# Delta stage: the seven-tap filter moved from VectorE to ScalarE and GpSimd, and the stage's order planned anew

## The reference, cut to what matters

```python
q, k, v = (silu(conv4(x @ W.T)) for each of the three)        # 4 heads of 32
delta_out = delta_rule_chunkwise(l2norm(q), l2norm(k), v * beta)   # chunks of 32 tokens
firs = [_dwconv_causal(vflat, f) for f in (fir_w3, fir_w7, fir_w15, fir_w31)]
branches = jnp.stack(firs + [v, delta_out], 0)                # six branches
stats = mean(abs(branches), -1)                               # one number per token, head, branch
h1 = gelu([x, stats] @ gate_w1.T + b1);  logits = h1 @ gate_w2.T + b2 + alpha * stats
probs = softmax(logits / temp) with a floor on the last branch
o = sum over branches of branch * prob;  o = rmsnorm(o);  x = x + o @ o_proj.T
```

## Time and profile before

| what | value |
|---|---|
| three executions | 3999.51, 4001.47, 4015.3 us (median 4001.47) |
| profiled execution, own time | 3997.58 us |
| its span | 3995.8 us, 88226 instructions |
| mean granted TensorE clock over the span | 0.865 |
| busy over the span | PE 82%, DVE 70%, ACT 58%, POOL 31% |

### The profile page before, as it was taken

One profiled execution on the slowest core, in us unless ns is written; L12 is line 12 of the kernel. 1 busy time (PEld: TensorE's weight loads), 2 busy tenths in 40 slices (PEclk: granted clock), 3 DMA queues, 4 the chain that ended last, 5 costly groups with the idle time before them and its releaser, 6 DMA issues. The chain is left out here.

```text
span 3995.8 us, 88226 instructions
## 1 busy us (share of the span) xinstructions
PE 3288.4 (82%) x36384; PEld 1507.5 (38%) x36384; DVE 2804.5 (70%) x4300; ACT 2329.8 (58%) x3893; POOL 1238.3 (31%) x1018
## 2 busy tenths in 40 slices
PE   5999999899767777699888888887995676876798
PEld 1222222266411112256533333333453555555444
DVE  8898899587689998887633776764436568657642
ACT  3888788676555555366432466665655565444564
POOL 1100100055447767555523000001003565453100
PEclk7999999899867778799989999997996676656799
DMA  4101010100010100100155011101000000000000
GB/s 100 28 9 28 19 22 4 36 2 2 11 32 16 32 16 16 48 1 2 27 61 68 18 30 30 33 23 52 1 1 11 4 4 3 4 4 3 30 1 22
DMA packets 138340, 85.14 MB, mean 21 GB/s; under 512 B 94578, under 2 KB 109731, under 8 KB 137811
## 3 DMA queue, kind: packets, MB, share of 16 engines
q1 hardware_dynamic: 135190, 75.24, 9.0%
q0 software_dynamic: 2688, 4.20, 0.7%
q10 hardware_dynamic: 64, 0.07, 0.0%
HBM read 47.49 MB, written 18.60 MB: 17 GB/s over the span
## 5 line engine op out<-in xcount | busy, mean ns | idle before, releaser
L949 DVE TENSOR_REDUCE attn_peak_halves<-attn_ps 128x2 f32<-128x1024 f32 x512 | 601.6, 1219 | 61.6 <-PE attn_ps L780 53.8
L902 ACT ACTIVATE attn_weights<-attn_ps 128x512 f32<-128x512 f32 x1024 | 531.1, 601 | 104.6 <-PE attn_ps L808 104.5
L2901 DVE TENSOR_REDUCE sparse_peak<-sparse_ps 128x4 f32<-128x1024 f32 x256 | 309.3, 1223 | 134.1 <-PE sparse_ps L2531 132.5
L1205 POOL TENSOR_TENSOR moe_hidden<-moe_exact,moe_hidden 128x512 f16<-128x512 f32 x256 | 297.0, 1164 | 329.3 <-ACT moe_hidden L1189 320.8
L3577 POOL TENSOR_TENSOR delta_q<-delta_q,delta_weighted 128x512 f32<-128x512 f32 x240 | 323.6, 1376 | 236.7 <-ACT delta_weighted L3971 236.3
L2761 ACT ACTIVATE sparse_weights<-sparse_ps 128x512 f32<-128x512 f32 (+1 forms) x512 | 272.0, 585 | 176.8 <-PE sparse_ps L2598 89.3
L246 PE MATMUL moe_ps<-moe_xT_halves,moe_w_halves 128*128 128x512 f16 x1536 | 363.6, 383 | 9.2 <-DVE moe_w_halves L1222 5.9
L808 PE MATMUL attn_ps<-attn_q_stack,attn_k_stack 50*128 50x512 f16 x1024 | 321.8, 386 | 33.7 <-ACT attn_weights L902 7.1
L1716 POOL TENSOR_TENSOR mamba_out_c<-mamba_states,mamba_c_rep 128x1024 f32<-128x1024 f32 x128 | 301.5, 2366 | 153.4 <-DVE mamba_states L1782 125.2
L246 PE MATMUL ffn_ps<-ffn_layers,ffn_h_halves 128*128 128x512 f16 x1536 | 334.5, 379 | 3.6 <-ACT ffn_gate L3130 3.6
L1506 PE MATMUL mamba_ps<-mamba_stack,mamba_spread 96*128 96x512 bf16 x512 | 197.3, 495 | 159.2 <-ACT mamba_decays L1670 85.0
(11 more groups left out here) (477 smaller groups left out, 6371.6 us busy)
## 6 DMA issues: line engine op xcount, KB each, us to landing
mamba_stack<-mamba_parts SPq DMA_DIRECT2D x96, 128.0 KB, 2.4
sparse_factor<-sp_factor SPq DMA_DIRECT2D x24, 256.0 KB, 3.8
sp_halves<-sparse_parts SPq DMA_DIRECT2D x8, 512.0 KB, 2.9
ffn_h<-in_h SPq DMA_DIRECT2D x4, 1024.0 KB, 7.7
attn_q_stack<-attn_halves SPq DMA_DIRECT2D x96, 32.0 KB
attn_k_stack<-attn_halves SPq DMA_DIRECT2D x96, 32.0 KB
attn_halves<-attn_hp SPq DMA_DIRECT2D x8, 384.0 KB, 3.3
attn_q_stack<-attn_peak_rows SPq DMA_DIRECT2D x128, 2.0 KB
```

The lines of the kernel that those rows point to most:

```text
L902: act.activation(weights[:, at % 2, h, :], use.slot, ACT.Exp).then_inc(*key_act.one())
L949: dve.tensor_reduce(peak_halves[:, turn % PEAKS, keys, at:at + 2], use.slot, AX_X, ALU.max).then_inc(*score_dve.one())
L1205: pool.tensor_tensor(low, exact_sb[:, i % 3, :], hidden[:, i // EB % 3, i % EB, 0, :], ALU.subtract).then_inc(*hidden_low.one())
L2901: dve.tensor_reduce(peak[:, at % PEAKS, unit // 2, 4 * r:4 * r + 4], use.slot.rearrange("p h (a k) -> p (h a) k", a=2), AX_X, ALU.max).the ...
```

## The change

The seven-tap filter (n = 1) leaves `TAP_ORDER`, so DVE makes the filters of 3 and 15 taps alone, 18 instructions for a sequence. `BY_POOL = (LONG, 1)` and `POOL_TAPS` put it behind the long filter in ACT's chain of scalings and POOL's chain of additions: 38 taps for a sequence in place of 31. Its first tap is written by ACT straight into `branch`, the other six go through `weighted` and POOL. The first scaling of the seven-tap filter waits for the last `sources` and the last absolute value of the sequence before. In `STAT_ORDER` branch 1 moves from the third place to the fifth. `URGENCY` goes from 0.004 to 0.002, and `AHEAD` gets other entries, so the order of all pieces of the stage is planned anew.

```diff
-TAP_ORDER = [(k, n) for k in range(max(FIR_TAPS)) for n, count in enumerate(FIR_TAPS) if n != LONG and k < count]
-STAT_ORDER = [4, 0, 1, 2, 3, 5]
+BY_POOL = (LONG, 1)
+POOL_TAPS = [(n, k) for n in BY_POOL for k in range(FIR_TAPS[n])]
+
+TAP_ORDER = [(k, n) for k in range(max(FIR_TAPS)) for n, count in enumerate(FIR_TAPS) if n not in BY_POOL and k < count]
+STAT_ORDER = [4, 0, 2, 3, 1, 5]
...
-URGENCY = 0.004
-AHEAD = {"kept": 1.5, "root": 1.5, "sums": 0.5, "norm_root": 0.5, "uw": 0.5, "raw": 2, "hidden": 0.5, "temper": -2, "o_scale": -0.5,
-         "values": -0.5, "apply": -2, "silu": -1, "turned": -0.5, "mix": -0.5, "moments": -0.5}
+URGENCY = 0.002
+AHEAD = {"moments": 4, "ruled": 2, "temper": 2, "lengthen": 1, "cross": 1, "turn": 1, "norm_root": 0.5, "silu": 0.5,
+         "apply": -0.5, "absolute": -0.5, "keep": -1}
...
+        scaled = [("scaled", b, i, half) for i in range(len(POOL_TAPS)) for half in range(HALVES)]
+        needs["scaled", b, POOL_TAPS.index((1, 0)), 0] += (
+            [("sources", b - 1, 1, TPC - 1), ("absolute", b - 1, 1, BRANCHES - 1)] if b else [("features", CHUNKS - 1)])
...
+        for n in BY_POOL:
+            needs["absolute", b, half, STAT_ORDER.index(n)] += [
+                ("long_tap", b, POOL_TAPS.index((n, FIR_TAPS[n] - 1)), HALVES - 1)]
...
-                    if p == LONG:
-                        act.wait_ge(*long_added.at(added_by(b)))
+                    if p in BY_POOL:
+                        act.wait_ge(*long_added.at(added_by(b, POOL_TAPS.index((p, FIR_TAPS[p] - 1)))))
...
+                    if k == half == 0 and n != LONG:
+                        if b:
+                            act.wait_ge(*wide_full.at(one("sources", b - 1, 1, TPC - 1).n))
+                            act.wait_ge(*absolute_made.at(means_made(b - 1)))
+                        else:
+                            act.wait_ge(*wide_full.at(one("features", CHUNKS - 1).n))
```

More of the change, by code:

```diff
@@ L3349, in delta_chains @@
         needs[taps[0]] += [("values", b)] + ([("sources", b - 1, 1, TPC - 1)] if b else [("features", CHUNKS - 1)])
[L3350 to L3359, removed]
+        scaled = [("scaled", b, i, half) for i in range(len(POOL_TAPS)) for half in range(HALVES)]
+        long_taps = [("long_tap",) + piece[1:] for piece in scaled if POOL_TAPS[piece[2]][1]]
+        needs[scaled[0]] += [("scale", b)] + ([("scaled", b - 1, len(POOL_TAPS) - 1, 1)] if b else [])
+        needs["scaled", b, POOL_TAPS.index((1, 0)), 0] += (
+            [("sources", b - 1, 1, TPC - 1), ("absolute", b - 1, 1, BRANCHES - 1)] if b else [("features", CHUNKS - 1)])
+        for n, piece in enumerate(long_taps):
+            needs[piece] += [("scaled",) + piece[1:]]
+            if n >= HALVES:
+                needs[("scaled",) + piece[1:]] += [long_taps[n - HALVES]]
+            elif b:
+                needs[("scaled",) + piece[1:]] += [("long_tap", b - 1, len(POOL_TAPS) - 1, piece[3])]
         chains += [taps, scaled, long_taps]
@@ L3377, in delta_chains @@
         needs["absolute", b, half, 1] += [("tap", b, len(TAP_ORDER) - 1)]
-        needs["absolute", b, half, 4] += [("long_tap", b, FIR_TAPS[LONG] - 1, HALVES - 1)]
+        for n in BY_POOL:
+            needs["absolute", b, half, STAT_ORDER.index(n)] += [
+                ("long_tap", b, POOL_TAPS.index((n, FIR_TAPS[n] - 1)), HALVES - 1)]
         needs["absolute", b, half, 5] += [("ruled", b, half)]
@@ L3560, in delta_stage, with added_by, made_by_pool @@
         means_made = lambda b: BRANCHES * HALVES * (b + 1)
-        added_by = lambda b, k=FIR_TAPS[LONG] - 1, half=HALVES - 1: (
-            HALVES * ((FIR_TAPS[LONG] - 1) * b + k - 1) + half + 1)
+        adding = [i for i, (n, k) in enumerate(POOL_TAPS) if k]
+        def added_by(b, i=len(POOL_TAPS) - 1, half=HALVES - 1):
+            return HALVES * (len(adding) * b + adding.index(i)) + half + 1
+        def made_by_pool(b, n, half):
+            return (long_of(b) if n == LONG else branch[:, n, :])[:, columns(half)]
         with nc.Block() as block:
@@ L3571, in _, with long_tap @@
             def _(pool):
-                def long_tap(b, k, half):
-                    so_far = long_of(b)[:, columns(half)]
-                    pool.wait_ge(*long_scaled.at(HALVES * (b * FIR_TAPS[LONG] + k) + half + 1))
+                def long_tap(b, i, half):
+                    n, k = POOL_TAPS[i]
+                    so_far = made_by_pool(b, n, half)
+                    pool.wait_ge(*long_scaled.at(HALVES * (b * len(POOL_TAPS) + i) + half + 1))
                     if k > 1:
-                        pool.wait_ge(*long_added.at(added_by(b, k - 1, half)))
+                        pool.wait_ge(*long_added.at(added_by(b, i - 1, half)))
                     pool.tensor_tensor(so_far, so_far, weighted[:, half, :], ALU.add).then_inc(*long_added.one())
@@ L3957, in stat_end, with scaled @@
                     made.then_inc(*stat_act.one())
[L3959 to L3962, removed]
+                def scaled(b, i, half):
+                    n, k = POOL_TAPS[i]
+                    at = HISTORY + k - FIR_TAPS[n] + 1 + half * BANK
+                    tap = sum(FIR_TAPS[:n]) + k
+                    if i == half == 0:
                         if b == 0:
@@ L3966, in scaled @@
                         act.wait_ge(*q_scaled.at(b + 1))
-                    if k > 1:
-                        act.wait_ge(*long_added.at(added_by(b, k - 1, half)))
+                    if k == half == 0 and n != LONG:
[4 more added lines that the diff above has]
+                            act.wait_ge(*wide_full.at(one("features", CHUNKS - 1).n))
+                    if k and adding.index(i):
+                        act.wait_ge(*long_added.at(added_by(b, adding[adding.index(i) - 1], half)))
                     elif k and b:
                         act.wait_ge(*long_added.at(added_by(b - 1, half=half)))
-                    act.activation(weighted[:, half, :] if k else long_of(b)[:, columns(half)],
+                    act.activation(weighted[:, half, :] if k else made_by_pool(b, n, half),
                                    v_all[:, b % 3, at:at + BANK], ACT.Copy,
```

## The result

Five executions of the changed kernel took 4025.21 to 4041.47 us, median 4038.7; five of the kernel before, on the same chip, 3991.11 to 4015.3 us, median 4001.47. The ratio is 1.0091, with a 95% interval of 1.0074 to 1.0109. The change makes the kernel slower by 0.9%, about 36 us, where I forecast 15 us faster; the result lies outside the range. The profiled execution took 4040.41 us.

What follows compares the result with a forecast made beforehand. The prediction took the delta stage's chain of tap and mixing stretches as the bound, with DVE busiest in the tap stretches. Terms -22.0 - 3.1 + 7 + 3 gave -15.1 us, a forecast of 3984 us, range 3955 to 4012.

Steps and rivals of the forecast that it cites:

- I take the share of the stretch in which DVE is busy: First three tap stretches: removed DVE taps count by DVE's busy share, 22.0 us of gain, ends 0 and 30.8.
- T3: Last sequence's stretch from first tap to first mean, 42.6 us before; a gain of 3.1 us taken, up to 8.7.
- 7 taken: ACT's added scalings in the delta stage delay the end by 7 us, the middle between nothing and 13.9.
- POOL and what it shares with DVE: Delta stage: POOL's 48 added additions stretch DVE's instructions through the shared port; cost taken as 3 us.
- The top of my range for the port: Upper end of the port cost, 13 us: the remaining 16 taps stretched by twice the present 0.27 us.
- the sum above: Delta stage's terms together: -22.0 - 3.1 + 7 + 3 = -15.1 us.
- The new order: 0 taken. Its ends are rivals.: Delta stage planned anew: the new order itself was counted at 0 us, its ends left to the rivals.
- The rival that the order packs better: Delta stage: fewer taps and another order free time, a gain of 30.5 us, 3967 us; chance 0.28.
- S0 to S3 at 66 to 69 us as now: Four mixing stretches, each from a sequence's first mean behind the taps, should stay at 66 to 69 us.
- The port takes it all: First three tap stretches bound by the port DVE and POOL share: DVE's relief worth nothing, 4003 us; chance 0.20.
- The hand-over ends last: ACT to POOL chain: twelve more additions, 27 us, push each next long filter; about 4025 us, chance 0.13.
- T1 and T2: Second and third sequences' stretches from first tap to first mean, each expected some 5 to 8 us shorter.

Runs made afterwards that it cites:

- the kept order: Seven-tap filter moved to ACT and POOL as in the change, all other pieces in the order of the kernel before; 4012.54 us, ratio 1.0027 against the kernel before.

## Why the prediction was wrong, point by point

**What bounds the kernel.** I read DVE's busy share in the tap stretches (63 to 90%) as the bound. The step "I take the share of the stretch in which DVE is busy" is the first that failed: with the taps gone and nothing put in their place, 6 us came off (1 to 11) and not 25.1. The busy share of an engine says how likely another instruction stands behind a tap, not that the late one is on the path. The nearer bound is PE's dependent products and the copies between them (40 us for 33 us more of PE); that a tap on DVE fell mostly into time in which PE had the other way's products to run is how I read it, not measured. In T3, where I had the full 8.7 us as the most, even the dropped taps gave 3.1 (39.5 for 42.6), and with the additions in the kept order T3 gave 0.4 (42.2).

**ACT.** 7 taken, 8 measured, with an interval of 0 to 16 us: the estimate is not contradicted.

**POOL and what it shares with DVE.** 3 taken. The added additions with their waits cost 19 us with all taps kept and, by the sums of the kept order (11 + 6 - 8), 9 us without the seven. The top of my range for the port was 13. Two things were too small in it: the taps stretched by 11 us where the additions were added and no taps removed, and ACT's wait for POOL grew from 57.4 to 86.7 us in the kept order (I said 65 to 75), which I had treated as a sign to look for and not as a price. ACT runs its list in order, so a wait to refill `weighted` can hold back copies for PE: PE's waits for ACT grew from 29.1 to 38.1 us in the kept order, though to 37.3 already by the scalings. Together the kept-order parts are +11 us where the sum above says -15.1.

**"The new order: 0 taken. Its ends are rivals."** This step cost the most. The order alone is worth some 26 us. Each of the two failures, this one and the relief (19 us less than counted), was enough to turn the sign of the forecast. The kernel held a number for it that I did not ask for: its own planner puts the end of the stage at 717.0 us before and at 727.1 with the change, 10.1 us later and not earlier. The rival that the order packs better was the only end I gave it, and that end was a gain. Nine orders planned anew, over both splits, were all slower than the kernel before, by 0.23% to 1.18%: there was no reason to give the new order a gain at 0.28 and a loss by it nothing. The profile of before held a hint too, in the 4.6 us that PE waits for DVE's copies over 7168 products: another order had little to win there.

**"S0 to S3 at 66 to 69 us as now."** Each lasted 11 to 15 us longer, and this is the second failed step, and mostly the order's (5 of the 51 us come with the order kept): I took them for a fixed chain of latencies, and even the dropped taps changed S0 by 6.5 and S2 by 4.4 us. In S3, where no other sequence is left, the part up to the second half's delta branch is 6.3 us longer (32.4 for 26.1) and the rest 5.8 (45.5 for 39.7); over both PE is busy 54.92 us for 48.02, so 6.9 of the 12.1 us are PE's, at a lower granted clock. S0 to S2 also carry more work of other sequences: PE is busy 64.4, 63.6 and 69.8 us there for 59.6, 61.9 and 61.0.

**The rivals.** *The port takes it all*, 4003 us with a chance of 0.20, is nearest to the kept order's 4012.5: the relief is worth about nothing and POOL's part costs. The page that I set against my forecast, the Trainium skill's Perfetto Trace Analysis (Optimizing Scalar/DVE Operations), that moving work between DVE and GpSimd might not help, came out right for the moved work; what this case adds is that even dropping the taps gave 6 us. *The hand-over ends last*, 4025 us, had the right sign, not the path. Sequence 3's long filter ended at 3656.7 us, which is past the 3647 that I had named, but the whole stretch had moved: it is 1.9 us after T3's start, where 3647 was 18. POOL's last addition (3691.1 us) was over 13 us before DVE's last tap, for which the mean waited. What POOL's part costs it costs in stretched taps and in waits along the stage.

**What held.** 288 additions, 72 taps, ACT's wait of 66.8 us (65 to 75 said), the first mean of T3 behind DVE. Not the taps in T3, of which I had said 1.5 us and more: they took 22.45 / 16 = 1.40 us there, and 24.28 / 16 = 1.52 in the first tap stretch:
```profile
3153.30:3244.50 91.20, 24.28 (x16) 0.63 0.02 4
3654.80:3704.50 49.70, 22.45 (x16) 0.57 0.01 3
```
T1 and T2 did shorten, by 20.8 us for the 10 to 16 expected. Had I looked at these alone, the change would have passed for a success; the stretches next to them gave back 51.

**What stays open.** What in an order lowers the granted clock (0.63 in four of the orders, 0.64 in one, 0.66 in the rest of the replanned ones), and so how the 26 us of the change's order divide between the clock and lost cover. Whether an order planned for a DVE without the seven taps would win more than 6 us was not run. No kernel of this study that computes all that the reference asks beats the kernel before.

## What to carry to other kernels

Before an engine's relief is counted, drop the work outright in a kernel that keeps the order of everything else: here that one kernel put a hope of 25 us at 6. When a planner or a list of weights is changed along with the work, treat the new order as a change of its own, with a loss at least as likely as a gain, ask the planner for its own end of both, and test it with the moved work in the old order. Crossing weights and work is a weaker test, since the planner then makes an order that suits neither. And measure a stage from end to end: a stretch that got shorter proves nothing while its neighbour can take it back.

## What the runs showed of the hardware that was not expected

The granted PE clock goes with the order of the same work: 17088 equal products kept PE busy 503 to 541 us over the kernels here, at 0.67 down to 0.63 in one profiled execution of each. It is not that execution alone: over the whole span the changed kernel's five executions had 0.858 to 0.861, the kernel before 0.865 to 0.872 in the 56 beside the experiments. From the first mean of sequence 3 to the end of the stage it stood at 0.54 with the change (77.9 us) and 0.66 before (65.8 us), and two 512-column products took 2.08 us in place of 1.13. Executions of one kernel differ the same way: in one set of 17 of the kernel before, 3983.6 us was reached at a granted clock of 0.872 over the span and 4007.7 at 0.867.
